# The MLP up product in pairs of sequences, as seven block products instead of eight

## The reference

```
h = _ln(x) * (1.0 + sc2) + sh2
h = gelu(h @ w1.T + b1)          # w1: 2048 x 512, the "up product"
x = x + g2 * (h @ w2.T + b2)     # w2: 512 x 2048, the "down product"
```

## Time and profile before

| what | value |
|---|---|
| median of 3 runs | 1443.88 us |
| span of the profiled execution | 1441.8 us |
| TensorE matmul busy | 1413.7 us (98%) |
| VectorE, ScalarE, GpSimd busy | 51%, 49%, 41% |
| DMA | 112.80 MB, mean 78 GB/s |

### The profile page before, as it was taken

How to read it: one execution, slowest core, us unless ns; L and a number is a source line. 1 busy time by engine, 2 the same in 40 slices (tenths; PEclk the granted TensorE clock), 3 DMA queues, 4 the chain that set the end, 5 groups by cost and what they waited for, 6 DMA issues and landing times.

```text
span 1441.8 us, 18434 instructions
## 1 busy us (share of the span) xinstructions
PE 1413.7 (98%) x6877; PEld 1023.2 (71%) x6877; DVE 733.8 (51%) x1293; ACT 708.4 (49%) x1275; POOL 585.3 (41%) x231
## 2 busy tenths in 40 slices
PE   6999999999999999999999999999999999999998
PEld 4655666666666665665578888888888888888887
DVE  3778777677777777687634522323122231321312
ACT  6377758576665757566734423323233232422321
POOL 3067587677858777687510111121201212012200
PEclk9999999999999999999999999999999999999999
DMA  7332322323232232324242321202112020121100
GB/s 281 90 86 56 100 66 82 111 85 109 77 116 54 79 103 86 118 77 116 91 130 88 81 94 30 95 3 64 59 30 95 19 83 24 30 95 30 66 0 30
DMA packets 99450, 112.80 MB, mean 78 GB/s; under 512 B 41033, under 2 KB 51289, under 8 KB 99361
## 3 DMA queue, kind: packets, MB, share of 16 engines
q1 hardware_dynamic: 99360, 111.62, 25.9%
HBM read 55.44 MB, written 16.81 MB: 50 GB/s over the span
## 4 chain that ended last, share of the span: by engine, by line
PE 90%; DVE 4%; ACT 2%; POOL 1%; DMA 1%; issue 1%; SPq 1%; DVEq 0%; ACTq 0%; POOLq 0%
PE acc L1733 24%; PE up L1486 24%; PE proj_bank L1153 14%; PE key_bank L1237 8%; PE pv_bank L1246 7%; PE row_bank L1224 7%; DVE neg_max L967 2%; PE sum_bank L1256 2%; POOL probs_sum L662 1%; PE turn L1470 1%; PE proj_bank L1163 1%; SPq L532 1%; ACT probs L791 1%; PE sum_bank L1292 1%; PE key_bank L1279 0%
## 5 line engine op out<-in xcount | busy, mean ns | idle before, releaser
L967 DVE TENSOR_REDUCE neg_max<-row_bank 128x1 f32<-128x512 f32 x512 | 337.5, 683 | 140.1 <-PE row_bank L1224 135.9
L791 ACT ACTIVATE probs<-key_bank 128x512 f32<-128x512 f32 x512 | 299.5, 597 | 160.0 <-PE key_bank L1237 158.1
L1486 PE MATMUL up<-h,w_t 128*128 128x512 f32 x1536 | 369.1, 390 | 0.0
L1733 PE MATMUL acc<-w_t,hidden 128*128 128x512 f32 x1536 | 367.8, 389 | 0.1
L1733 PEld LDWEIGHTS acc<-w_t,hidden 128*128 128x128 f32 x1536 | 288.2, 188 | 60.3 <-DVE hidden L1679 0.5
L1679 DVE TENSOR_TENSOR hidden<-up,hidden 128x512 fp32r<-128x512 f32 x128 | 88.5, 691 | 474.8 <-ACT hidden L1616 474.8
L1486 PEld LDWEIGHTS up<-h,w_t 128*128 128x128 f32 x1536 | 287.3, 188 | 59.0
L1607 ACT ACTIVATE up<-up,bias_cols 128x512 f32<-128x512 f32 x128 | 84.7, 662 | 446.3 <-PE up L1486 446.3
L662 POOL TENSOR_TENSOR probs_sum<-probs_sum,probs 128x2048 f32<-128x2048 f32 x62 | 285.5, 4605 | 14.2 <-ACT probs L791 7.3
L1237 PE MATMUL key_bank<-q_stack,k_stack 128*128 128x512 f32 x512 | 217.2, 427 | 3.3 <-ACT probs L791 2.8
L1224 PE MATMUL row_bank<-k_stack,q_stack 96*128 96x512 f32 x512 | 203.4, 408 | 3.7 <-DVE neg_max L967 2.2
(11 more groups left out here) (153 smaller groups left out, 1122.7 us busy)
## 6 DMA issues: line engine op xcount, KB each, us to landing
q_stack<-spare SPq DMA_DIRECT2D x384, 64.0 KB, 2.0
xa<-in_x_dram SPq DMA_DIRECT2D x8, 1024.0 KB, 9.8
resid<-in_x_dram SPq DMA_DIRECT2D x8, 1024.0 KB, 7.0
x_scratch<-resid SPq DMA_DIRECT2D x8, 1024.0 KB, 4.5
xa<-x_scratch SPq DMA_DIRECT2D x8, 1024.0 KB, 5.5
spare<-in_L_cond_w_dram SPq DMA_DIRECT2D x32, 256.0 KB, 3.1
resid<-x_scratch SPq DMA_DIRECT2D x8, 1024.0 KB, 7.4
out_dram<-y SPq DMA_DIRECT2D x7, 1024.0 KB, 4.2
```

What stands on the lines that cost most here:

```text
L791: nc.scalar.activation(probs[kt][:, r, :], key_bank[r % 2][:, :], ACT.Exp).then_inc(exp_done, 1)
L967: nc.vector.tensor_reduce(out=neg_max[:, g % 2, i:i + 1], in_=row_bank[(g + i) % 2][:, :], op=ALU.max, axis=AX.X, negate=True).then_inc(ro ...
L1486: last = nc.tensor.matmul(up[j % 2][:, :], w_t[:, j, i, kt * P:kt * P + P], h[k][:, kt, :], start=(kt == 0 and n == 0), stop=(kt == KD - 1 ...
L1733: last = nc.tensor.matmul(acc[tt][:, :], hidden[j % 2][i][:, tt * P:tt * P + P], w_t[:, j, 2 + k, :], start=(j == 0 and n == 0), stop=(j = ...
```

## The change

Sequences 0 and 1 go through the MLP as before, sequences 2 to 7 in three pairs (c = 1 to 3). For a pair the weight w1 is cut in 2 x 2 blocks (row tile j and j + 8; two halves of the contraction) and the activations in 2 x 2 blocks (two halves of the contraction; two sequences). Per block row jp (0 to 7) seven products of 6 matmuls each are made (`product`), where four up products of 12 matmuls stood. Four of the seven use sums of weight blocks, and four use sums of activation blocks.

- Weight sums: during sequence 1 GpSimd forms four block sums for each jp, ScalarE and VectorE split them, and SyncE stores them to DRAM (`w1s_dram`). The unmixed blocks are stored there during sequence 0.
- Ring: in the pairs each product's weights (256 KB) are loaded by SyncE into one of eight buffers (`RING_SLOTS`), which lie where the up weights of `w_t` were. The load of product g waits for product g - 8.
- Activation sums: `mix` on VectorE, `mix_high` on ScalarE, `mix_low` on VectorE, during the end of sequence 1 or the second phase of the pair before.
- Combining: per jp one copy on ScalarE (`copy_p1`) and five additions on VectorE (`combine`: U2, U3, C22, C21, C12), in PSUM and SBUF.
- Order of a pair: in phase A the products are made and the first sequence's down products run among them; the hidden tiles of the second sequence wait in SBUF or go to DRAM (`store_b`). In phase B 16 down products of the second sequence run one after the other, with `load_b`.
- Both sequences of the next pair are made ready in phase A. In `second` (sequence 1) those of the first pair are.
- SyncE no longer waits for the end of a result's store before it issues the loads behind it.

The core of the diff:

```diff
+S2, S1, S3, S4, A11, A12, A22 = range(NQ)
+BLOCK_OF = (S2, A11, S3, S1, A12, A22, S4)
+BLOCKS = 2 * JP + JP
+RING_SLOTS = ((2, 0), (2, 1), (13, 0), (13, 1), (14, 0), (14, 1), (15, 0), (15, 1))
...
+SUMS_AT = (2, 4, 5, 7, 9, 11, 12, 14)
...
+        q_bank = [up[1], up[0], turn[0], turn[1], up[0], turn[0], turn[1]]
...
+            def load_product(g):
+                jp, q = g // NQ % JP, g % NQ
+                r = g % len(ring)
+                if g < len(ring):
+                    sp.wait_ge(up_ready, NJ + RING_SLOTS[r][0] + 1)
+                    sp.wait_ge(a_ready, 2 * JP)
+                    sp.wait_ge(blocks_stored, BLOCKS * 16)
+                else:
+                    sp.wait_ge(product_done, g - len(ring) + 1)
+                if g < JP * NQ:
+                    sp.wait_ge(s_stored, (jp + 1) * 64)
+                sp.dma_start(as_f32(ring[r][:, :, :, :]).rearrange("p a i f -> p (a i f)"),
...
+            def second():
+                sp.wait_ge(h_split, KD)
+                load_x(2)
+                store(0)
+                load_out_parts(1)
+                store_sums(0)
+                sp.wait_ge(up_ready, NJ + 2)
+                sp.wait_ge(a_ready, 4)
+                sp.wait_ge(blocks_stored, BLOCKS * 16)
+                load_x(3)
+                store_sums(1)
+                turn_halves(2)
+                store_sums(2)
+                store_sums(3)
+                turn_halves(3)
+                for jp in range(4, JP):
+                    store_sums(jp)
+                for g in range(len(ring)):
...
+            def pair(c, has_next):
+                first = product_no(c, 0, 0) + len(ring)
+                last = product_no(B // 2 - 1, JP - 1, NQ - 1)
+                for jp in range(JP):
+                    if jp == 0:
+                        store(2 * c - 1)
+                        load_out_parts(2 * c)
+                        if has_next:
+                            sp.wait_ge(mix_split, c * len(MIXED))
+                            load_x(2 * c + 2)
+                            load_x(2 * c + 3)
+                    for q in range(NQ):
+                        if first + jp * NQ + q <= last:
+                            load_product(first + jp * NQ + q)
+                        if q == 3 and has_next and jp in (3, 5):
+                            turn_halves(2 * c + (2 if jp == 3 else 3))
+                        if q == 4 and 2 * jp < NJ - 4:
+                            store_b(c, 2 * jp)
+                        if q == 1 and 0 < jp and 2 * jp - 1 < NJ - 4:
+                            store_b(c, 2 * jp - 1)
+                for n in range(NJ - 4):
+                    if n == 4:
+                        store(2 * c)
+                        load_out_parts(2 * c + 1)
+                    load_b(c, n)
+                if not has_next:
+                    store_tiles(2 * c + 1)
...
+            def mix_weights(jp):
+                lo, hi = slice(0, HALF), slice(HALF, N)
+                s21, s34 = [as_f32(t[:, :]) for t in s_tile]
+                pool.wait_ge(a_ready, 2 * jp + 2)
+                if jp > 0:
+                    pool.wait_ge(s_stored, 64 * jp)
+                nc.gpsimd.tensor_tensor(s21[:, hi], a_tile[1][:, lo], a_tile[1][:, hi], ALU.add).then_inc(s_ready, 1)
+                nc.gpsimd.tensor_tensor(s34[:, lo], a_tile[0][:, lo], a_tile[1][:, lo], ALU.subtract).then_inc(s_ready, 1)
+                pool.wait_ge(s_ready, 4 * jp + 1)
+                nc.gpsimd.tensor_tensor(s21[:, lo], s21[:, hi], a_tile[0][:, lo], ALU.subtract).then_inc(s_ready, 1)
+                pool.wait_ge(s_ready, 4 * jp + 3)
+                nc.gpsimd.tensor_tensor(s34[:, hi], a_tile[0][:, hi], s21[:, lo], ALU.subtract).then_inc(s_ready, 1)
...
+                for jp in range(JP):
+                    whole(jp)
+                    mix_weights(jp)
+                    if jp == 0:
+                        next_rstd(2)
+                    if jp == 2:
+                        bias_resid(1)
+                    if jp == 3:
+                        next_rstd(3)
+                add_out(1, range(TT))
...
+            def copy_p1(c, jp):
+                act.wait_ge(product_done, product_no(c, jp, 1) + 1)
+                if c > 1 or jp > 0:
+                    act.wait_ge(combined, combined_no(c, jp, "C12") - len(COMBINED))
+                else:
+                    act.wait_ge(s_stored, 64 * JP)
+                nc.scalar.activation(p1, up[0][:, :], ACT.Copy).then_inc(p1_copied, 1)
...
+            def second():
+                for j in range(NJ):
+                    gelu(1, j)
+                    hidden_high(1, j, False)
+                    if j in SUMS_AT:
+                        sums_high(SUMS_AT.index(j))
+                    if j == 2:
+                        norm_next(2)
+                    if j == 6:
+                        for kt in range(KD):
+                            modulate_next(2, kt)
+                        norm_next(3)
...
+            def second():
+                for j in range(NJ):
+                    hidden_low(1, j)
+                    if j in SUMS_AT:
+                        sums_low(SUMS_AT.index(j))
+                    if j == 0:
+                        tile_stats(2)
+                    if j == 1:
+                        next_moments(2)
+                    if j == 2:
+                        next_shift(2)
+                    if j == 3:
+                        for tt in range(TT):
+                            halve(2, tt)
+                    if j == 4:
+                        x_stats(3)
+                    if j == 5:
+                        next_moments(3)
+                        for kt in range(KD):
+                            join(2, kt)
+                    if j == 6:
+                        next_shift(3)
+                    if j == 7:
+                        for tt in range(TT):
+                            halve(3, tt)
+                    if j == 8:
+                        copy_cond(3)
+                    if j == 9:
+                        for kt in range(KD):
+                            join(3, kt)
+                    if 11 <= j:
+                        for n in range(4 * j - 44, min(4 * j - 40, MIX_EARLY)):
+                            mix_step(1, n)
...
+                r = g % len(ring)
+                if jp == 0 and q == 0:
+                    pe.wait_ge(mix_split, mix_no(c, 1, 1))
+                    if c == 1:
+                        pe.wait_ge(hid_split, 2 * NJ)
+                    else:
+                        pe.wait_ge(b_gelu, b_tile_no(c - 1, NJ - 2))
+                if jp == 0 and q in (4, 6):
+                    pe.wait_ge(mix_split, mix_no(c, q, 1))
+                if jp > 0 and q == 0:
+                    pe.wait_ge(b_gelu, b_tile_no(c, 2 * jp - 2))
+                if jp > 0 and q in (1, 2):
+                    pe.wait_ge(pair_split, pair_no(c, 2 * jp - 3 + q))
+                if jp > 0 and q == 3:
+                    pe.wait_ge(b_gelu, b_tile_no(c, 2 * jp - 1))
+                if q == 4:
+                    pe.wait_ge(p1_copied, (c - 1) * JP + jp + 1)
+                if q == 5:
+                    pe.wait_ge(combined, combined_no(c, jp, "U3"))
+                if q == 6:
+                    pe.wait_ge(combined, combined_no(c, jp, "C22"))
+                pe.wait_ge(ring_loaded[r], 16 * (g // len(ring)) + 16)
+                for i in range(2):
+                    for n, (a, k) in enumerate(PASSES):
+                        last = nc.tensor.matmul(q_bank[q][:, :], ring[r][:, a, i, :], moving(q, i, k),
+                                                start=(q < 4 and i == 0 and n == 0), stop=(i == 1 and n == 2),
+                                                skip_group_check=True)
+                last.then_inc(product_done, 1)
...
+            def pair(c, has_next):
+                for jp in range(JP):
+                    product(c, jp, 0)
+                    product(c, jp, 1)
+                    if jp > 0:
+                        pair_product(c, 2 * jp - 2, jp - 1)
+                    product(c, jp, 2)
+                    product(c, jp, 3)
+                    if jp > 0:
+                        pair_product(c, 2 * jp - 1, jp - 1 + JP)
+                    product(c, jp, 4)
+                    product(c, jp, 5)
+                    product(c, jp, 6)
+                pair_product(c, NJ - 2, JP - 1)
+                pair_product(c, NJ - 1, NJ - 1)
+                for m in range(NJ):
+                    n = tile_of(m)
+                    pair_product(c, NJ + m, n // 2 + (0 if n % 2 else JP))
```

More of the change, by code:

```diff
@@ new lines, in mlp, with sequences @@
+        ring_loaded = [sem(f"ring_loaded{r}") for r in range(len(ring))]
+        b_stored, b_loaded = [sem(f"b_stored{n}") for n in range(4)], [sem(f"b_loaded{n}") for n in range(4)]
+        product_done, p1_copied, combined = sem("product_done"), sem("p1_copied"), sem("combined")
```

(40 more changed lines are left out.)

539 lines of the change are left out of this document (422 added, 117 removed).

## The result

The changed kernel took 1460.14 us (median of 4 runs, 1458.84 to 1461.24), beside 1443.74 for the kernel before on the same chip: a ratio of 1.0114, 95% interval 1.0099 to 1.0128. Slower, as forecast, but by 16.4 us where 5 were forecast, and just outside the range. The profiled execution has a span of 1457.3 us and took 1459.29 us.

The account below looks back on a forecast made before the run. The prediction took TensorE, busy 98%, to bound the kernel: 1441.8 - 32.6 + 26.3 + 6.7 + 4.5 = 1446.7 us of span, and with the runs' median 2.1 above it 1448.8 us; range 1434 to 1459.

Parts of the forecast that it names:

- Removed, and the steady part: Three pairs: 144 fewer matmuls save 32.6 us; additions and copy hide in each 14.96 us jp, costing 0.
- The start of a pair: Product 8's load waits in SyncE's queue behind store, gate, residual and x: stalls 12.6, 9.7 and 4.0, +26.3 us.
- The first rival: At the pairs' start, ring loads aren't held up, and start and clock terms vanish: 1418 us, chance 0.12.
- Sequence 1 (`second`), +6.7: Sequence 1, readying two sequences beside weight sums, has late tiles at 6, 7 and 10: +6.7 us, bounds 3 to 12.
- eight joins 2.9: Sequence 1: VectorE's eight joins after sequence 2's transposes take 2.9 us, putting tile 6's low part at 41.0.
- The stall at down(6): Sequence 1: tile 6's low part, behind transposes and joins, comes at 41.0 where 38.1 was due: 2.9 us.
- the 2.9 forecast at down(7): Sequence 1: `next_rstd(3)` and ScalarE's normalisation delay GELU 7; split at 49.3, due at 46.4: 2.9 us.
- The clock: Half clock behind the stalls at the three pairs' starts: 1.8, 1.8 and 0.9, +4.5 us, bounds 0 and 6.
- the rest of the sequence holds: Sequence 1 beyond the late tiles 6, 7 and 10: no further stall; VectorE has at most 4.8 of 5.44 us.
- the forecast's own upper bound of 12: Sequence 1's cost if GpSimd's half-width additions take 1.28 us, with `next_rstd(3)` 4.4 later: 12 us.
- GpSimd's price: Sequence 1's weight sums: a half-width GpSimd addition, shown by no row, was taken as 0.65 us.
- The third rival: Half-width GpSimd additions over about 0.9 us make sequence 1's sums, power and normalisation late: 1455 to 1460 us, chance 0.17.

Follow-up runs that it names:

- both reordering runs: Changed kernel with SyncE's loads of products 8 to 10 first: 1430.28 us; changed kernel with only the next pair's x loads moved behind the ring loads: 1451.53 us.
- narrow sums: Changed kernel with GpSimd's six weight-sum instructions per block row on 8 columns instead of 512 and 256 (sums wrong): 1452.46 us.
- best version: Third try: the second with sequence 1's bias earlier in 128-column instructions, fifth and seventh sums a tile later, last sums after the last tile: 1423.98 us, ratio 0.9862.
- first of the three tries: Changed kernel with the loads of products 8 to 10 first and GpSimd's weight sums cut into 128-column instructions: 1431.03 us, ratio 0.9911.
- second: The first of the three tries with sequence 1 reordered: sequence 2's transposes and sequence 3's power earlier, sequence 3's joins and some sums later: 1428.26 us, ratio 0.9898.
- both together: Changed kernel with weight sums on 8 columns (sums wrong) and the ring's loads first: 1419.97 us beside 1444.28.
- x later: Changed kernel with only the next pair's x loads (2 MB) moved behind block row 0's ring loads; store, gate and residual stay ahead: 1451.53 us.

## Why the prediction was wrong

**Removed, and the steady part: right.** 144 matmuls at 0.2267 us; the jp is 14.96 us long; phase B is packed, but for one gap each in pairs 1 and 2 (0.35 and 0.28).

**The start of a pair: right.** The chain of waits of the changed kernel names each link, from GpSimd's last additions to product 8:

```profile
934.87 3.80 POOL y L1774 x3
...
938.69 0.39 SPq L1637
...
943.47 10.78 DMA ring<-w1s_scratch
...
954.38 2.90 PE up L2304 x6
```

The store is issued at +6.4 (forecast 6.9) and product 8 starts at +22.1 (forecast 23.5); for c = 2 and 3 the store stands at +4.1 (3.9). The stalls were 11.09, 8.32 and 3.50, forecast 12.6, 9.7 and 4.0. From the store's issue to product 8 it took 15.7, 15.3 and 10.4 us where the forecast had 16.6, 16.6 and 10.9; in a window of pair 3's stall the queue moves 404 GB/s. The close sum of the three pairs (30.3 for 30.8) is luck in part: the stalls are 3.4 shorter than forecast, and 2.7 of small gaps and overlap that the forecast didn't have stand against them. The first rival, in which product 8 passes what stands ahead of it, is out, and moving the loads ahead took the stalls to zero. The Trainium skill ("DMA: Bandwidth & Descriptors", Queues, rings and completion order) has descriptors consumed in ring order; both reordering runs agree, 5.6 us for the 2 MB that no longer stood ahead.

**Sequence 1 (`second`), +6.7: the step that failed.** Its terms "eight joins 2.9" and, by the same row, the eight halves ahead of the transposes were mis-sized: measured 7.18 and 6.05. The earlier trace rows were read in the kernel before, where GpSimd does nothing beside those copies. The forecast moved GpSimd's sums beside them and asked only whether GpSimd would be in time, not what its work does to VectorE's. From there the loss can be followed: the halves end 3.2 later, so that SyncE starts the transposes 29.5 from the sequence's start and not 25.7; they land at 41.2 and not 37.4; the joins take 4.3 longer; and the low part of tile 6 is ready at 48.9 where 41.0 was forecast. Each stall costs 0.2 to 0.3 more than its idle time, read from group start to group start. So counted, the 9.7 close:

- The stall at down(6) costs 10.1 and not 2.9: +7.2.
- It swallows the 2.9 forecast at down(7): -2.9. That the power and normalisation of sequence 3 were late, as forecast, can't be seen behind it.
- The clock: +1.8 behind the long stall (4.65 for twelve matmuls in place of 2.88), which the forecast charged only to the pairs.
- Stalls at down(4), down(13) and down(15) (0.51, 0.26 and 1.66 idle), where the forecast had "the rest of the sequence holds": +3.4; down(10) +0.2. None of the first three is in the run with narrow sums, so they too come from GpSimd's sums; how much of them is VectorE's slower work and how much sums that come late isn't separated.

The +16.4 lies beyond the forecast's own upper bound of 12, which had GpSimd's price in it and nothing for its neighbours. With the sums narrow the same low part was ready at 40.9, and sequence 1 took 93.3 us where 93.7 was forecast. That last agreement is luck in part, as a half clock of 1.7 stands there in place of most of the 2.9 at down(7).

The Trainium skill ("SBUF — State Buffer", Who interferes with whom) states this rule: one pair of ports is shared by VectorE and GpSimd, held by one of them for its whole instruction, and the other waits; VectorE needs it for a copy in its two-port mode and for an operation with two SBUF inputs, and not for one with a single SBUF input outside that mode. The runs agree, though no view here tells the mode of a copy: copies went from 0.35 to 1.1 us and two subtractions of SBUF tiles from 1.28 to 3.46 beside the bias, the operation with a PSUM operand stayed at 691 ns, and the wait was shorter behind shorter instructions. This page bore on the change more than the one that the forecast weighed.

**GpSimd's price: right, and no matter.** The half-width addition costs 0.73 to 0.75 us where nothing disturbs it and up to 0.99 beside VectorE's copies; 0.65 was taken. The third rival, which needed 0.9, gave a time near the result for a cause that didn't occur.

**The clock: near in the pairs (4.7 for 4.5), wrong in where it applies.** By the starts of the matmuls behind it the first stall cost 2.6 (they took 2.90 and 4.18 where 1.52 and 2.88 are usual), the second 2.1 (2.90, and the 3.63 of the line below) and the third 0.1. The forecast had 1.8, 1.8 and 0.9, and nothing for sequence 1, where it was 1.8. That the third cost none was a case and no rule, as the last section shows.

```profile
1132.37 3.63 PE L2317 MATMUL acc<-w_t,hidden 128*128 128x512 f32 x12
```

**Open.** In the best version's 11 us, the clock (4.4) and the stall at down(7) (3.4, GpSimd late) are told apart. The rest, mostly the stall at down(15), ends as VectorE's hidden tile, and how much of it is waiting for the ports and how much GpSimd's own loop isn't separated. Sums formed without GpSimd weren't tried.

## What to carry to other kernels

- Work put on an idle engine has two prices: its own time, and what it does to its neighbours. Before moving element-wise work to GpSimd, list the VectorE instructions that will run beside it, and separate copies and operations with two SBUF inputs from those that read PSUM.
- A queue in order is a schedule. When new just-in-time loads share it with megabyte transfers, put the first deadline first: here one order of the same DMAs was worth 30 us, of which 23 were stalls and 5 the half clock behind them.
- After a stall is found, ask what it covers. Three tries at sequence 1 each gained less than the stall that they shortened, as the next item was already late.

## What the runs showed of the hardware

Windows of the changed kernel in the stall at product 8 of pair 1, behind it, and in that of pair 3, with the same columns as the window above:

```profile
945.00:947.00 2.00, 0.00 (x0) 0.00 (x0) 0.00 (x0) 0.00 (x0) 1.02 (x1) 0.79 0.95 328
957.00:959.00 2.00, 2.00 (x6) 1.53 (x5) 1.05 (x3) 0.60 (x1) 0.00 (x0) 0.50 1.09 356
...
1297.00:1299.00 2.00, 0.00 (x0) 0.00 (x0) 0.00 (x0) 0.00 (x0) 0.37 (x1) 1.00 1.05 404
```

The granted clock falls to 0.50 (1.2 GHz) in the stall and is still there when the matmuls are back; it returns within the next twelve. In pair 3, after a stall of 3.50 us, it stays at 1.00 and the matmuls have full speed. In the run with narrow sums it was down behind a stall of only 2.75 us, by this window:

```profile
871.00:873.00 2.00, 2.00 (x7) 1.55 (x7) 0.16 (x1) 0.65 (x1) 1.45 (x4) 0.61 0.00 0
```

All stalls between 2 and 4 us in the traces from sequence 1 on, with what the matmuls behind them lost, by their starts (stalls of at most 1.7 us lost no more than 0.2):

| stall, us | run | lost, us |
|---|---|---|
| 2.23 | first of the three tries | 1.7 |
| 2.28 | second | 0.2 |
| 2.49 | third | 1.6 |
| 2.74, 2.75 | both together; narrow sums | 1.7, 1.7 |
| 3.22 | third | 2.8 |
| 3.33, 3.61 | x later | 2.8, 2.8 |
| 3.47 | narrow sums, pair 3 | 1.7 |
| 3.50 | changed kernel, pair 3 | 0.1 |

Stalls of 5.46 to 11.09 us cost 1.6 to 2.8. So the length of the stall doesn't decide: from 2.2 to 3.6 us the rows show both outcomes, and what decides is open. In a sum such a stall has a bound of 0 and one of 2.8.

GpSimd loses as well where the two meet: four additions of the bias took 5.75 us beside VectorE's subtractions and first join, 5.01 in the earlier trace rows.
